# Retrieval stage of a four-layer block: first one-hots on two engines, first splits on GpSimd, index row ahead of a transfer

## The reference, cut to what matters

```python
s1, i1 = top_k(sim1, 8); s2, i2 = top_k(sim2, 8)      # 4 heads, keys of 128 halves
final_scores, pk_idx = top_k(s1[:, None] + s2[None, :], 8)
final_indices = take(i1 * 128 + i2, pk_idx)           # 32 of 4096 experts a token
hidden = silu(einsum('btd,bthkd->bthk', x, e_down[final_indices])) * relu(final_scores)
out = einsum('bthk,bthkd->btd', hidden, e_up[final_indices])
x = x + tanh(g_ffn[3]) * out
```

## Time and profile before

| | us |
|---|---|
| three runs | 1835.58, 1837.11, 1837.71 (median 1837.11) |
| profiled execution, its time | 1835.21 |
| profiled execution, its span | 1833.4 |
| TensorE, VectorE, ScalarE, GpSimd busy | 1331.3, 1511.1, 869.8, 556.4 |
| mean granted clock of TensorE | 0.859 of full |

### The profile page before, as it was taken

How to read it: one execution, slowest core, us unless ns; L and a number is a source line. 1 busy time by engine, 2 the same in 40 slices (tenths; PEclk the granted TensorE clock), 3 DMA queues, 4 the chain that set the end, 5 groups by cost and what they waited for, 6 DMA issues and landing times. The chain is left out here.

```text
span 1833.4 us, 23885 instructions
## 1 busy us (share of the span) xinstructions
PE 1331.3 (73%) x6398; PEld 990.5 (54%) x6398; DVE 1511.1 (82%) x3239; ACT 869.8 (47%) x1726; POOL 556.4 (30%) x573
## 2 busy tenths in 40 slices
PE   4799228886999417444474199069999899998888
PEld 2354114444888303134341188057888788877776
DVE  5999378985877698799759789797899898988885
ACT  3455356662333141154331143136888788843443
POOL 0000005443110141400005013302576666666651
PEclk8999669997999755766585599589999999999999
DMA  5010420000000400155201010223688788888985
GB/s 172 23 35 1 189 75 1 0 0 1 1 1 1 129 23 0 46 162 171 92 0 41 1 46 24 69 51 115 213 242 253 232 245 259 247 249 250 277 238 156
DMA packets 91355, 198.41 MB, mean 108 GB/s; under 512 B 14856, under 2 KB 24200, under 8 KB 90384
## 3 DMA queue, kind: packets, MB, share of 16 engines
q0 software_dynamic: 27120, 91.25, 18.0%
q1 hardware_dynamic: 64160, 106.34, 17.3%
HBM read 181.81 MB, written 15.73 MB: 108 GB/s over the span
## 5 line engine op out<-in xcount | busy, mean ns | idle before, releaser
L2229 POOL DMA_INDIRECT L3f_gd<-rows,idx x160 | 181.0, 1131 | 204.8 <-DVE L3f_gd L2458 180.8
L2229 POOL DMA_INDIRECT L3f_gu<-in_L_ffn_e_up,idx x160 | 167.1, 1045 | 71.3 <-issue 47.2
L2297 PE MATMUL L3f_o_ps<-L3f_euh,L3f_ath 128*128 128x512 f32 x352 | 145.4, 413 | 15.9 <-DVE L3f_atl L2439 15.9
L2285 PE MATMUL L3f_h_ps<-L3f_xh,L3f_edh 128*128 128x512 f32 (+1 forms) x384 | 144.6, 376 | 8.2 <-DVE L3f_xl L2444 8.2
L926 POOL TENSOR_TENSOR L0f_hq<-L0f_hid,magic 128x1408 bf16<-128x1408 f32 x16 | 45.2, 2824 | 338.9 <-DVE L0f_hid L997 338.9
L2285 PE MATMUL L3f_h_ps<-L3f_xl,L3f_edh 128*128 128x512 f32 (+1 forms) x384 | 144.2, 375 | 0.0
L2285 PE MATMUL L3f_h_ps<-L3f_xh,L3f_edl 128*128 128x512 f32 (+1 forms) x384 | 144.2, 375 | 0.0
L2269 PE MATMUL L3f_g_ps<-L3f_oh 128*128 128x128 f32 x704 | 97.5, 283 | 62.7 <-DVE L3f_oh L2426 62.7
L2297 PE MATMUL L3f_o_ps<-L3f_euh,L3f_atl 128*128 128x512 f32 x352 | 137.6, 391 | 0.0
L2297 PE MATMUL L3f_o_ps<-L3f_eul,L3f_ath 128*128 128x512 f32 x352 | 137.5, 391 | 0.0
L2269 PEld LDWEIGHTS L3f_g_ps<-L3f_oh 128*128 128x128 f32 x704 | 91.3, 194 | 73.3 <-issue 68.8
(11 more groups left out here) (526 smaller groups left out, 3702.3 us busy)
## 6 DMA issues: line engine op xcount, KB each, us to landing
L3f_eu<-in_L_ffn_e_up SPq DMA_DIRECT2D x96, 256.0 KB, 4.8
L3f_ed<-in_L_ffn_e_down SPq DMA_DIRECT2D x96, 256.0 KB, 4.5
L2x_ed<-in_L_ffn_e_down SPq DMA_DIRECT2D x32, 256.0 KB, 3.4
rows<-L2x_eo SPq DMA_DIRECT2D x32, 256.0 KB, 2.4
ternary_wgu<-in_L_ffn_w_gate_upT SPq DMA_DIRECT2D x4, 1408.0 KB, 10.4
X<-in_x SPq DMA_DIRECT2D x4, 1024.0 KB, 10.6
L0x_V<-in_ctxT SPq DMA_DIRECT2D x8, 512.0 KB, 3.8
L1f_C<-in_ctx SPq DMA_DIRECT2D x2, 2048.0 KB, 12.6
```

The source lines that it names most:

```text
L2229: pool.indirect_dma_start(buf[j % ND][:, :], None, table, bass.IndirectOffsetOnAxis(ap=idx[:, j:j + 1], axis=0)).then_inc(sem[j % ND], 16)
L2285: last = pe.matmul(h_ps[h][:, 0:cols], lhsT=w[h][:, c, :], rhs=x[:, c, 0:cols], start=(c == 0 and m == 0), stop=(c == DC - 1 and m == 2))
L2297: last = pe.matmul(o_ps[a][:, :], lhsT=w[h][:, a * P:(a + 1) * P], rhs=x[h][:, :], start=False, stop=False)
```

## The change

Four things are edited. A fourth of the small one-hots of groups 0 to 31 (the last of each four) is made on ScalarE by `last_hot(i)`, with new counters `last_far` and `last_made`, and TensorE waits for `last_made` as well; VectorE makes three. ScalarE's keeps of pair i-1 stand behind `last_hot(i)` in its queue. The low parts of experts 0 and 1 and of the first tokens are subtracted by GpSimd, behind the first ten gathers. On GpSimd the index row and the zeros come ahead of the transfer of `xc`, and VectorE makes `xs` in the middle of the head (after 16 groups) instead of ahead of it.

```diff
--- before.py
+++ after.py
@@ -2188,6 +2188,7 @@
     edh_ready, edl_ready, euh_ready, eul_ready = (ph.pair_sem(n) for n in ("edh", "edl", "euh", "eul"))
     h_ready, sl_ready, at_ready, ath_ready, atl_ready, used = (ph.pair_sem(n) for n in ("h", "sl", "at", "ath", "atl", "used"))
     oh_ready, g_ready, G_ready = (ph.pair_sem(n) for n in ("oh", "g", "G"))
+    last_made, last_far = ph.pair_sem("last"), ph.pair_sem("last_far")
     minus_ready, far_ready, oh1_ready = ph.sem("minus"), ph.sem("far"), ph.sem("oh1")
     gd_in, gu_in = [ph.sem(f"gd_in{k}") for k in range(ND)], [ph.sem(f"gu_in{k}") for k in range(ND)]
     xs_ready, dotted, hid_ready, coef_ready, added = (ph.sem(n) for n in ("xs", "dotted", "hid", "coef", "added"))
@@ -2228,14 +2229,23 @@
                 pool.wait_ge(used, j - ND + 1)
             pool.indirect_dma_start(buf[j % ND][:, :], None, table, bass.IndirectOffsetOnAxis(ap=idx[:, j:j + 1], axis=0)).then_inc(sem[j % ND], 16)
 
-        pool.dma_start(xc[:, :, :], xT_dram[0]).then_inc(xc_in, 16)
         pool.iota(io[:, :], pattern=[[1, P]], base=0, channel_multiplier=0, allow_small_or_imprecise_dtypes=True).then_inc(io_made, 1)
         pool.memset(zero[:, :], 0.0).then_inc(zeroed, 1)
+        pool.dma_start(xc[:, :, :], xT_dram[0]).then_inc(xc_in, 16)
         up_rows = A["L3_ffn_e_up"].rearrange("e p c -> (e p) c")
         for j in range(ND):
             gather(rows_dram[:, :], gd, gd_in, dotted, j)
         for j in range(ND):
             gather(up_rows, gu, gu_in, added, j)
+        def low(out, whole, high, sem, value, done):
+            pool.wait_ge(sem, value)
+            pool.tensor_tensor(out, whole, high.bitcast(F32), ALU.subtract).then_inc(done, 1)
+
+        low(eul[0][:, :], eu[0][:, :], euh[0][:, :], euh_ready, 3, eul_ready)
+        for h in range(2):
+            low(edl[h][:, :, :], ed[h][:, :, :], edh[h][:, :, :], edh_ready, h + 3, edl_ready)
+        for c in range(DC):
+            low(xl[:, c, :], xc[:, c, :], xh[:, c, :], xh_ready, c + 1, xl_ready)
         for q in range(NQ):
             for k in range(NP):
                 if k == 1 and q < NQ - 1:
@@ -2305,6 +2315,7 @@
         pe.wait_ge(zeroed, 1)
         with pe.Fori(0, NP) as i:
             for h in range(2):
+                pe.wait_ge(last_made, here(i, h))
                 weigh(2 * i + h, h)
         for q in range(NQ):
             pe.wait_ge(xl_ready, DC * (q + 1))
@@ -2324,7 +2335,7 @@
 
     @block.scalar
     def _(act):
-        count_from_two(act, edh_ready, euh_ready, sl_ready, ath_ready, G_ready)
+        count_from_two(act, edh_ready, euh_ready, sl_ready, ath_ready, G_ready, last_made, last_far)
         def down_high(n, h):
             act.wait_ge(ed_in[h], 16 * (n // 2) + 16)
             act.wait_ge(h_ready, n + 1)
@@ -2362,6 +2373,20 @@
                 last = act.activation(oh1[h][:, g, :], oh1[h][:, g, :], ACT.Relu, scale=minus[:, n * GR + g:n * GR + g + 1],
                                       bias=first[:, 1, n * GR + g:n * GR + g + 1])
             last.then_inc(oh1_ready, 1)
+
+        def last_hot(i):
+            for h in range(2):
+                at_g = bass.ds((2 * i + h) * GR + GR - 1, 1)
+                act.wait_ge(g_ready, before(i, h))
+                act.activation(oh1[h][:, GR - 1, :], io[:, :], ACT.Abs, scale=-1.0, bias=first[:, 0, at_g]).then_inc(last_far, 1)
+            for h in range(2):
+                at_g = bass.ds((2 * i + h) * GR + GR - 1, 1)
+                act.wait_ge(last_far, here(i, h))
+                act.activation(oh1[h][:, GR - 1, :], oh1[h][:, GR - 1, :], ACT.Relu, scale=minus[:, at_g], bias=first[:, 1, at_g]).then_inc(last_made, 1)
+
+        def keep_two(i):
+            for h in range(2):
+                keep(2 * i + h, 0, i, h)
 
         def hidden_units(q, k):
             at = [q, k - 1] if k else [q - 1, NP - 1]
@@ -2397,31 +2422,38 @@
 
         act.wait_ge(zeroed, 1)
         act.activation(one[:, :], zero[:, 0:1], ACT.Silu)
+        act.wait_ge(io_made, 1)
         act.wait_ge(minus_ready, 1)
+        last_hot(0)
+        last_hot(1)
+        keep_two(0)
         up_high(0, 0)
         for h in range(2):
             down_high(h, h)
+        last_hot(2)
+        keep_two(1)
         for q in range(NQ):
             act.wait_ge(xc_in, 16 * q + 16)
             act.wait_ge(h_ready, q * EB + 2)
             for c in range(DC):
                 act.activation(xh[:, c, :], xc[:, c, :], ACT.Copy).then_inc(xh_ready, 1)
             if q == 0:
-                with act.Fori(0, NP) as i:
-                    for h in range(2):
-                        keep(2 * i + h, 0, i, h)
+                with act.Fori(3, NP) as i:
+                    last_hot(i)
+                    keep_two(i - 1)
+                keep_two(NP - 1)
             for k in range(NP):
                 turn(q, k, q < NQ - 1 or k < NP - 1)
 
     @block.vector
     def _(dve):
         count_from_two(dve, edl_ready, eul_ready, at_ready, atl_ready, oh_ready)
-        def one_hots(n, h, both_sides=True):
+        def one_hots(n, h, firsts):
 
             dve.wait_ge(g_ready, n + 1)
             last = dve.tensor_tensor(oh2[h][:, :, :], io[:, :].unsqueeze(1).to_broadcast([P, GR, P]),
                               second[:, bass.ds(n * GR, GR)].unsqueeze(2).to_broadcast([P, GR, P]), ALU.is_equal)
-            for g in range(GR if both_sides else 0):
+            for g in range(firsts):
                 at_g = bass.ds(n * GR + g, 1)
                 last = dve.tensor_scalar(oh1[h][:, g, :], io[:, :], first[:, 0, at_g], first[:, 1, at_g], ALU.is_equal, ALU.mult)
             last.then_inc(oh_ready, 1)
@@ -2489,29 +2521,30 @@
             gathered(js[:1])
             low(n + 1, 1, cols)
             if more:
-                one_hots(n + EB + 2, 0, False)
+                one_hots(n + EB + 2, 0, 0)
             if ahead:
                 down_low(n + 3, 1)
             gathered(js[1:2])
             if more:
-                one_hots(n + EB + 3, 1, False)
+                one_hots(n + EB + 3, 1, 0)
             if ahead:
                 up_low(n + 2, 0)
             gathered(js[2:])
 
         dve.tensor_scalar(minus[:, :], first[:, 1, 0:NO * GR], -1.0, None, ALU.mult).then_inc(minus_ready, 1)
         dve.wait_ge(io_made, 1)
-        up_low(0, 0)
-        for h in range(2):
-            down_low(h, h)
-        split_x(0)
+        with dve.Fori(0, NP // 2) as i:
+            for h in range(2):
+                one_hots(2 * i + h, h, GR - 1)
         for t in range(NG):
             dve.tensor_scalar(xs[:, t, :], X[:, TG + t, :], stat[:, 0, t:t + 1], stat[:, 1, t:t + 1],
                               ALU.subtract, ALU.mult).then_inc(xs_ready, 1)
+        with dve.Fori(NP // 2, NP) as i:
+            for h in range(2):
+                one_hots(2 * i + h, h, GR - 1)
         dve.wait_ge(xs_ready, NG)
-        with dve.Fori(0, NP + 1) as i:
-            for h in range(2):
-                one_hots(2 * i + h, h)
+        for h in range(2):
+            one_hots(2 * NP + h, h, GR)
         for q in range(NQ):
             dve.wait_ge(G_ready, min((q + 1) * EB, NO) + 2)
             for k in range(NP):
```

## The result

| | before | after |
|---|---|---|
| median of the runs | 1836.34 us (1835.55 to 1837.71) | 1859.94 us (1858.00 to 1863.34) |
| profiled execution, its span | 1833.4 us | 1859.0 us |
| start of `minus` on VectorE | 1181.07 us | 1181.86 us |
| first weigh on TensorE | 1198.55 us | 1185.15 us |
| first expert matmul | 1250.86 us | 1272.19 us |

The kernel became slower: ratio 1.0129 [1.0116, 1.0143]. The first weigh comes 13.4 us earlier, and all of it and 21 us more is lost before the first expert matmul. The span grew by 25.6: 0.8 ahead of `minus`, 20.5 in the head, 4.3 behind it.

A forecast was written before the change was run, and what follows sets the result against it. It took the head, then TensorE, to set the pace: 14.9 us saved ahead of the first weigh, slower pairs, head end +14.4, cold expert matmuls +1.5, together +16: 1853 us by the median, range 1834 to 1863.

The forecast's parts named there:

- the serial chain of TensorE and ScalarE: Head loop: TensorE idles once a pair while ScalarE works; with a falling clock 1844 to 1863 us, chance 0.60, (3) included.
- the sum of 16: Whole kernel: head end +14.4 us plus +1.5 behind it, together +16, 1851.2 on the profiled execution.
- First weigh: Start of the head: TensorE's first weigh at 1183.65 instead of 1198.55, 14.9 us saved.
- The step of 0.13: Ahead of a TensorE matmul: time from an end on VectorE or ScalarE to the matmul it releases, 0.13 us.
- The pause: Head loop: TensorE idle 1.94 us once a pair, for release, Abs, two Relu, keep and release; bounds 1.74 and 2.6.
- The clock: Head loop: 24% of the time at 2.4 GHz, the rest at 1.2, so a pair takes 5.18 us.
- The edit costed at nothing: Seven low halves on GpSimd: may slow VectorE 0 to 4 us, slack 1.1 us a pair, so taken as 0.
- Behind the head: After the head: expert matmuls begin at the low clock for some 3 us, costing half of that, +1.5.
- (1): Rival, head loop: the clock holds, pairs at 3.98 us, -1.4 and 1835.7 by the median; chance 0.27.
- (2): Rival, head loop: ScalarE's chain is hidden and VectorE's 1.44 us a group decides, -18.5, 1818.6; chance 0.10.
- (3): Rival, head loop: low clock throughout or a longer pause, +24.6, 1861.7; chance included in the serial chain's 0.60.
- (4): Rival, head start: something on ScalarE's way holds the first weigh; with held clock +3 to +8; chance 0.03.

The follow-up runs named there:

- e8: Changed kernel without small one-hots on ScalarE (VectorE makes four), the seven low halves on VectorE in one block with `xs` mid-head; ratio to before 0.9996, head 69.2 us.
- e2: Changed kernel with only ScalarE's order altered: keep, Abs and Relu of one group, then of the other; ratio to before 0.9999, head 69.4 us.
- e5: Changed kernel run again unaltered, on another set's chip; ratio to before 1.0114, head 87.7 us.
- e4: Changed kernel plus four bf16 matmuls on zeros behind each pair of weighs, filling TensorE's pause; ratio to before 1.0059, head 78.6 us.
- e1: Changed kernel with GpSimd's low halves 2 to 7 each waiting for an odd VectorE group, not in a row; ratio to before 1.0101, head 84.3 us.
- e9: e2 with the seven low halves on VectorE, these and the five `xs` one to a pair in pairs 4 to 15; ratio to before 0.9943, head 58.1 us.

## Why the prediction came out as it did

The forecast was 1853 with 1834 to 1863, by the serial chain of TensorE and ScalarE with a clock that keeps falling. That mechanism is what happened; the measured loss, 25.6 us of span, is 9.6 over the sum of 16.

- **First weigh.** Predicted 1183.65, measured 1185.15. 0.8 of it is the stage, which began later. 0.7 is the term itself: ScalarE's first Relu ends near 1184.3 and TensorE starts 0.85 later. The row names VectorE's second group as releaser, but e8, without ScalarE's share, starts TensorE 3.18 us after `minus` as well (1179.02 to 1182.20, released by "issue"), 1.13 after VectorE's first group is done. In all thirteen profiles with the early start the first weigh comes 3.17 to 3.29 us after `minus`. So something other than the one-hots sets it; no run shows what. The step of 0.13 after the last input was wrong here, by little.
- **The pause.** Predicted 1.94, measured 1.85 in nearly every pair, and named as the keep `L3f_G`. Right, down to the order of its parts; e2 shows that order and not amount of work makes it.
- **The clock.** Predicted 24% of the time at 2.4 GHz, measured 0.65 as mean in 1210 to 1250, which is 30%. Twelve pairs from 1208.94 to 1268.75 take 4.98 each, against 5.18. The size came from one row of another stage with TensorE half busy, not from a law, and that it came so near is partly luck: in e5 the same kernel has 0.71 there, which is 42%. The Trainium skill (TensorE: Matmul & The Clock Gate, "Why this matters for your kernels") advises against idle gaps longer than these; keeping below them did not suffice here, for with a dozen gaps of 1.85 us the clock kept falling, and e4, with the gaps filled down to 0.98 us, has 1.00 from 1210 on.
- **The edit costed at nothing.** This is the step that was mis-sized: "GpSimd may slow VectorE ... between 0 and 4 us ... and VectorE has 1.1 us of slack a pair, so 0". It measured 7.7 us: the first three pairs take 23.8 instead of 16.1 (22.8 in e5). The error was to treat the overlap as a slowdown that slack absorbs. The trace shows a hold: one small one-hot stands until GpSimd's chain of seven is over, and TensorE idles 7.96 us; in e5 VectorE gets one instruction in for each of the last four subtractions. The Trainium skill (SBUF — State Buffer, "SBUF: two separate sides") tells this of one instruction: where a VectorE operation needs the port pair that it shares with GpSimd, the engine that starts first has the pair for all of its instruction and the other blocks. Four profiles agree in kind: the held instruction ends 0.08 to 0.10 us behind a subtraction in after, e1, e2 and e5. In after and e2 the hold goes further than one instruction, over all seven.
- **Behind the head.** Predicted +1.5 from a first round that begins at the low clock; that round takes 209.9 us in both kernels, so the term is not there. Measured +4.3 (2.4 in the second round, 1.9 in the third). The second round alone scatters by more than that between profiles of one code, so no cause is claimed.
- **The rivals.** (1), the clock holds, was refuted in this kernel, and e4 shows it where the pauses are filled. (2), VectorE's 1.44 a group decides, needed another order on ScalarE; with it (e2) a pair takes 3.0, near the 2.87 given, but by ScalarE, whose work the prediction put at 2.33 a pair: keep, Abs and Relu follow each other in steps of about 0.50 us, six to a pair. (3), low clock throughout, 1861.7, was nearest in time and for the wrong reason: 30% of the stretch was at the high clock, and the stall filled the difference. (4) did not show: ScalarE's splits ran from 1190.99 without a wait.

The sum of the misses: 0.8 + 0.7 + 7.7 - 2.6 (pairs and `xs`) + 0.2 (the last pair) + 2.8 = 9.6.

## What to carry to other kernels

When work is moved to an engine that also drains the buffers of the next step, write down its queue for one loop turn beside the other engines': if each consumer's turn lies wholly between two of the producer's bursts, the loop is a relay, and its price is the sum of the steps plus the clock that TensorE loses in the pauses. Order can cost more than amount: the same instructions gave 90 and 69 us. Work that nobody waits for yet is cheapest one piece to a turn, in the slack of the loop; as a block it was on the path in each place tried here: ahead of the loop, in its middle, and on GpSimd beside it.

## What the runs showed of the hardware that was not expected

- Seven GpSimd subtractions of 128x512 in a row kept a VectorE instruction of about 0.3 us waiting until they were over (9.35 us, in after and in e2); in e5 VectorE got one instruction in for each of the last four, the small ones at 1.3 us apiece. One such subtraction beside a large one-hot made it 1.72 us instead of 0.69. On GpSimd a low half takes 1.27 us, on VectorE 0.68.
- TensorE in bursts of 16 records (2.05 us at the full clock) with pauses of 1.85 us keeps falling to 1.2 GHz and rising again; in bursts of 8 records (1.15 us) with pauses of 0.2 to 0.9 us (e9 from 1200 on) it stays at 2.4 GHz.
- With the one-hots first, TensorE's first matmul of the stage comes 3.2 to 3.3 us after `minus` starts, whichever engines make its input (thirteen profiles); what sets this is open.
- ScalarE and VectorE waited 1.5 to 6.8 us at about 1191 to 1198, with no releaser on the core, in six of the profiles; the cause is open.
